# Value product of the attention from rounded parts, early products of the output projection, and a later output-weight load

## The reference, cut to what matters

```python
qkv = nodes @ Wqkv.T + bqkv                      # 512 x 2304
q, k, v = jnp.split(qkv, 3, axis=-1)             # 8 heads of 96
scores = jnp.einsum('nhd,mhd->hnm', q, k)        # q scaled by 96 ** -0.5
probs = jax.nn.softmax(scores, axis=-1)          # 8 x 512 x 512
attn = jnp.einsum('hnm,mhd->nhd', probs, v).reshape(n, D)
attended = attn @ Wo.T + bo
return nodes + attended                          # then x + this, layer norm, experts
```

## Time and profile before

| | us |
|---|---|
| three runs | 1343.64, 1342.67, 1346.37 (median 1343.64) |
| profiled execution, its own time | 1343.39 |
| span from its first to its last instruction | 1341.8 |
| mean granted TensorE clock in it | 0.989 |
| PE busy | 1276.1 (95%) |
| DVE busy | 918.2 (68%) |
| ACT busy | 589.3 (44%) |
| POOL busy | 127.7 (10%) |

### The profile page before, as it was taken

One profiled execution on the slowest core, in us unless ns is written; L12 is line 12 of the kernel. 1 busy time (PEld: TensorE's weight loads), 2 busy tenths in 40 slices (PEclk: granted clock), 3 DMA queues, 4 the chain that ended last, 5 costly groups with the idle time before them and its releaser, 6 DMA issues. The chain is left out here.

```text
span 1341.8 us, 19527 instructions
## 1 busy us (share of the span) xinstructions
PE 1276.1 (95%) x7089; PEld 1107.3 (83%) x7090; DVE 918.2 (68%) x1837; ACT 589.3 (44%) x1022; POOL 127.7 (10%) x123
## 2 busy tenths in 40 slices
PE   5999999999999999999999999999999898899997
PEld 4777569969969996666999999999998778796864
DVE  6477573473473475556759999999998778837524
ACT  3011141351351244235418888898886227502110
POOL 0000200000000000003320000000003018600101
PEclk9999999999999999999999999999999998999799
DMA  9421190410410620003257999999998300008134
GB/s 338 171 93 33 55 359 10 153 71 1 153 71 1 235 96 0 1 24 141 100 210 295 346 391 386 386 398 377 384 391 286 119 29 1 1 1 294 46 108 165
DMA packets 80704, 225.48 MB, mean 168 GB/s; under 512 B 5184, under 2 KB 17024, under 8 KB 80512
## 3 DMA queue, kind: packets, MB, share of 16 engines
q1 hardware_dynamic: 72736, 187.64, 37.8%
q0 software_dynamic: 7904, 36.97, 7.7%
HBM read 197.85 MB, written 26.74 MB: 167 GB/s over the span
## 5 line engine op out<-in xcount | busy, mean ns | idle before, releaser
L2149 DVE TENSOR_TENSOR part_slot<-slot,item_hi 128x768 fp32r<-128x768 f32 x150 | 133.1, 948 | 0.2
L1579 ACT ACTIVATE item_hi<-slot 128x768 fp32r<-128x768 f32 x156 | 118.0, 833 | 24.0 <-DMA slot<-in_e0w 22.5
L2158 DVE TENSOR_TENSOR part_slot<-slot,item_hi 128x768 fp32r<-128x768 f32 x132 | 116.5, 951 | 2.0 <-ACT item_hi L1587 1.5
L1587 ACT ACTIVATE item_hi<-slot 128x768 fp32r<-128x768 f32 x132 | 99.2, 831 | 13.9 <-DMA slot<-in_e0w 13.9
L731 PE MATMUL dve_ps<-item_hi,x_hi 128*128 128x384 f32 x288 | 99.3, 345 | 0.5 <-DVE x_lo L2338 0.3
L731 PE MATMUL act_ps<-item_hi,hid_hi 128*128 128x384 f32 x288 | 98.4, 342 | 0.3 <-DVE hid_lo L2350 0.3
L733 PE MATMUL dve_ps<-item_hi,x_lo 128*128 128x384 f32 x288 | 97.2, 337 | 0.0
L732 PE MATMUL act_ps<-part_slot,hid_hi 128*128 128x384 f32 x288 | 96.8, 336 | 0.0
L733 PE MATMUL act_ps<-item_hi,hid_lo 128*128 128x384 f32 x288 | 96.1, 334 | 0.0
L732 PE MATMUL dve_ps<-part_slot,x_hi 128*128 128x384 f32 x288 | 95.7, 332 | 0.0
L1470 ACT ACTIVATE h_t<-act_ps,par 128x256 f32<-128x256 f32 x36 | 21.1, 587 | 121.6 <-PE act_ps L849 121.6
(11 more groups left out here) (419 smaller groups left out, 3302.6 us busy)
## 6 DMA issues: line engine op xcount, KB each, us to landing
slot<-in_e0w SPq DMA_DIRECT2D x48, 2304.0 KB, 10.6
slot<-in_w SPq DMA_DIRECT2D x9, 2304.0 KB, 8.7
experts<-in_e1w SPq DMA_DIRECT2D x8, 1152.0 KB, 15.5
ea_raw<-in_edge SPq DMA_DIRECT2D x8, 1024.0 KB, 5.4
slot<-in_wqkv SPq DMA_DIRECT2D x3, 2304.0 KB, 13.7
xs<-zrow POOLq DMA_DIRECT2D x2, 3072.0 KB, 15.7
item_x<-xs SPq DMA_DIRECT2D x16, 384.0 KB, 9.7
ys<-item_y POOLq DMA_DIRECT2D x16, 384.0 KB, 6.9
```

The lines of the kernel that those rows point to most:

```text
L1579: go(item_hi[j][k][:, :], slot[s][:, k * D:(k + 1) * D], ACT.Copy).then_inc(up_high[j], 1)
L1587: go(item_hi[j][k][:, :], slot[s][:, k * D:(k + 1) * D], ACT.Copy).then_inc(down_high[j], 1)
L2149: vv.tensor_tensor(part_slot[s][:, ks], slot[s][:, ks], item_hi[j][k][:, :].bitcast(F32), ALU.subtract).then_inc(up_low[j], 1)
L2158: vv.tensor_tensor(part_slot[s][:, ks], slot[s][:, ks], item_hi[j][k][:, :].bitcast(F32), ALU.subtract).then_inc(down_low[j], 1)
```

## The change

1. The values are kept as two halves of four heads (`v`, in slot 0), rounded by ACT (`high_v`) and subtracted by DVE (`low_v`). The turned probabilities are also kept in parts: ACT copies all four banks into `prb_hi`, DVE subtracts that from the same bank into `prb_lo`, and it is DVE's subtraction that frees the bank. `weigh` makes 12 matmuls in fp32r in place of 4 plain ones, and waits bank by bank.
2. In heads 6 and 7 all four turned banks come from the ACT ring. The two `spend` calls there go. In head 6 PE makes 4 matmuls on ones and blocks 0 to 2 of unit 2, in head 7 blocks 0 to 2 of units 3 and 0, all ahead of `turn_probs`.
3. `high_attn`/`low_attn` of blocks 0 to 2 move into head 5 (behind ACT's four copies, behind DVE's `maxima(6)`).
4. `high_out` moves from behind the copies of the turned banks to right behind the exponentials of heads 5 and 6.
5. The whole output weight is loaded into slot 1 once query block 5 is made, in two pieces of 1152 KB; its rounded blocks lie in six places of their own (`wo_hi`).
6. `probs` has one buffer in place of two. Block 5 of the first expert's first half is rounded and subtracted last, after the output projection and after the norm.

```diff
-    HEAD_ACT, HEAD_DVE = HEAD_ACT + 2, HEAD_DVE + 2
+    HEAD_ACT, HEAD_DVE = (HEAD_ACT + 2, HEAD_DVE + 2) if _i < NH - 2 else (HEAD_ACT + NT, HEAD_DVE)
...
-            load(0, sview(0, 4, D), kview(wo[0:4 * P, :]))
...
             sp.wait_ge(sig.to_dve, DVE0["heads"] + HEAD_UNIT["q5"] + 1)
-            load(0, slot[0][:, 4 * D:DC * D].rearrange("p (k n) -> p k n", k=2), kview(wo[4 * P:DC * P, :]))
+            load(1, sview(1, DC, D)[:, 0:3, :], kview(wo[0:3 * P, :]))
+            sp.dma_start(sview(1, DC, D)[:, 3:DC, :], kview(wo[3 * P:DC * P, :])).then_inc(in_wo, 16)
...
             def turn_probs(i):
-                if i >= NH - 2:
-                    spend(act_bank(HEAD_UNIT[f"turn_a{i}"], a0), (10, 16)[i - NH + 2])
                 pe.wait_ge(prob_set, NT * (i + 1))
...
             def weigh(i):
-                pe.wait_ge(sig.act_freed, a0 + HEAD_UNIT[f"turn_a{i}"] + 2)
-                pe.wait_ge(sig.dve_freed, v0 + HEAD_UNIT[f"turn_v{i}"] + 2)
+                half, at = hd // 4, hd % 4 * DH
+                pe.wait_ge(v_low, half + 1)
                 for m in range(NT):
-                    last = mm(bank[0:DH, :], v[:, m, hd * DH:(hd + 1) * DH], prb_t[:, m, :], start=(m == 0), stop=(m == NT - 1))
+                    if i >= NH - 2:
+                        pe.wait_ge(sig.act_freed, a0 + HEAD_UNIT[f"turn_a{i}"] + m + 1)
+                    elif m % 2 == 0:
+                        pe.wait_ge(sig.act_freed, a0 + HEAD_UNIT[f"turn_a{i}"] + m // 2 + 1)
+                    else:
+                        pe.wait_ge(sig.dve_freed, v0 + HEAD_UNIT[f"turn_v{i}"] + m // 2 + 1)
+                    last = mm_parts(bank[0:DH, :], (v_hi[:, half, m, at:at + DH], v_lo[:, half, m, at:at + DH]),
+                                    (prb_hi[:, m, :], prb_lo[:, m, :]), start=(m == 0), stop=(m == NT - 1))
...
+                if i == NH - 2:
+                    spend(dve_ps[2], 4)
+                    pe.wait_ge(sig.dve_freed, v0 + HEAD_UNIT[f"turn_v{i - 1}"] + 2)
+                    attended(2, range(3), True)
+                if i == NH - 1:
+                    pe.wait_ge(sig.dve_freed, v0 + HEAD_UNIT[f"pv{i - 2}"] + 1)
+                    attended(3, range(3))
+                    pe.wait_ge(sig.dve_freed, v0 + HEAD_UNIT[f"pv{i - 1}"] + 1)
+                    attended(0, range(3))
                 turn_probs(i)
...
+            attended(2, range(3, DC - 1), True)
+            attended(3, range(3, DC - 1))
+            attended(0, range(3, DC - 1))
+            pe.wait_ge(sig.dve_freed, DVE0["wo"])
+            attended(used_last, range(DC - 1))
+            pe.wait_ge(wo_low, DC)
+            pe.wait_ge(attn_low, DC)
             for u in range(RING):
                 attended(u, range(DC - 1, DC)).then_inc(sig.to_dve, 1)
...
             for i in range(NH):
                 for t in range(NT):
...
+                if i in (5, 6):
+                    high_out(range(3 * (i - 5), 3 * (i - 4)))
                 for name in BETWEEN[i].split():
                     if name[0] == "k":
                         key(int(name[1]))
-                for j in range(2):
-                    go(prb_t[:, 2 * j, :], bank[:, :], ACT.Copy).then_inc(sig.act_freed, 1)
-                if i in (5, 6):
-                    high_out(range(3 * (i - 5), 3 * (i - 4)))
+                for m in range(NT):
+                    go(prb_hi[:, m, :], bank[:, :], ACT.Copy).then_inc(probs_high, 1)
+                if i == 0:
+                    high_v(1)
+                if i == 5:
+                    for k in range(3):
+                        high_attn(k)
...
-            for j in range(2):
-                high_up(j, 0)
+            high_up(0, 0, blocks=range(DC - 1))
+            high_up(1, 0)
+            act.wait_ge(sig.to_dve, DVE0["wo"] + 8)
+            high_up(0, 0, blocks=(DC - 1,))
...
             maxima(0)
+            low_v(0)
             for i in range(NH):
...
-                    vv.tensor_copy(prb_t[:, 2 * j + 1, :], bank[:, :]).then_inc(sig.dve_freed, 1)
+                for m in range(NT):
+                    dve.wait_ge(probs_high, NT * i + m + 1)
+                    vv.tensor_tensor(prb_lo[:, m, :], bank[:, :], prb_hi[:, m, :].bitcast(F32), ALU.subtract).then_inc(freed, 1)
                 if i + 1 < NH:
                     maxima(i + 1)
+                if i == 0:
+                    low_v(1)
+                if i == 5:
+                    for k in range(3):
+                        low_attn(k)
...
-            low_up(0, 0)
+            low_up(0, 0, range(DC - 1))
...
+            low_up(0, 0, (DC - 1,))
             keep_turned(run0, xn1_t)
...
                 pool.wait_ge(wo_high, k + 1)
-                nc.gpsimd.tensor_tensor(part_slot[0][:, ks], slot[0][:, ks], part_slot[1][:, ks].bitcast(F32), ALU.subtract
+                nc.gpsimd.tensor_tensor(part_slot[1][:, ks], slot[1][:, ks], wo_hi[k][:, :].bitcast(F32), ALU.subtract
```

More of the change, by code:

```diff
@@ L241, in build @@
         h_lo = over("h_lo", [P, DC, N], 18432, F32R)
-        v = over("v", [P, NT, D], 12288)
+        v = place("v", [P, 2, NT, HALF], F32, 0)
+        v_lo = place("v_lo", [P, 2, NT, HALF], F32R, 0)
+        v_hi = over("v_hi", [P, 2, NT, HALF], 12288, F32R)
         attn_t = over("attn_t", [P, DC, N], 6144)
@@ L257, in build @@
                  enumerate([3072, 3072 + D, cpt_at + 2 * N, area + 21504, area + 2048, bc_at])]
-        prb = over("prb", [P, 2, NT, N], 15360)
-        prb_t = over("prb_t", [P, NT, N], 19456)
+        prb = over("prb", [P, NT, N], 15360)
+        prb_lo = over("prb_lo", [P, NT, N], 17408, F32R)
+        prb_hi = over("prb_hi", [P, NT, N], 19456, F32R)
+        wo_hi = [place(f"wo_hi{k}", [P, D], F32R, at) for k, at in
+                 enumerate([3072, 3072 + D, 0, D, cpt_at + 2 * N, area + 22784])]
         xn1 = over("xn1", [P, NT, D], 0)
@@ new lines, in weigh, with attended @@
+                last.then_inc(sig.to_dve, 1)
+            def attended(u, ks, first=False):
+                t, half = u // 2, u % 2
+                ts, hs = slice(t * P, (t + 1) * P), slice(half * HALF, (half + 1) * HALF)
+                for k in ks:
+                    if first:
+                        pe.wait_ge(wo_low, k + 1)
+                        pe.wait_ge(attn_low, k + 1)
+                    last = mm_parts(dve_ps[u % RING][:, 0:HALF], (attn_hi[:, k, ts], attn_lo[:, k, ts]),
+                                    (wo_hi[k][:, hs], kslot(1, D, True)[:, k, hs]), start=(k == 0), stop=(k == DC - 1))
+                return last
@@ L1533, in _, with high_v @@
                 go(part_slot[3][:, k * D:(k + 1) * D], slot[2][:, k * D:(k + 1) * D], ACT.Copy).then_inc(w_high, 1)
+            def high_v(half):
+                act.wait_ge(sig.dve_freed, DVE0["v"] + 7 + half)
+                go(v_hi[:, half, :, :], v[:, half, :, :], ACT.Copy).then_inc(v_high, 1)
+            high_v(0)
             def key(b):
@@ L1559, in _, with high_up @@
                         key(int(name[1]))
-                for j in range(2):
-                    bank = bank_of(HEAD_UNIT[f"turn_a{i}"] + j, a0)
-                    wait(act, sig.to_dve, DVE0["heads"] + HEAD_UNIT[f"pv{i - 1}"] + 1 if i else 0)
-                    go(prb_t[:, 2 * j, :], bank[:, :], ACT.Copy).then_inc(sig.act_freed, 1)
-                if i in (5, 6):
-                    high_out(range(3 * (i - 5), 3 * (i - 4)))
-            act.wait_ge(sig.to_act, ACT0["heads"] + HEAD_UNIT["k5"] + 1)
-            for k in range(DC):
-                act.wait_ge(sig.dve_freed, DVE0["heads"] + HEAD_UNIT[f"pv{NH - 2 if k < DC - 1 else NH - 1}"] + 1)
-                go(attn_hi[:, k, :], attn_t[:, k, :], ACT.Copy).then_inc(attn_high, 1)
-            def high_up(j, i, home=None, before=0):
+                wait(act, sig.to_dve, DVE0["heads"] + HEAD_UNIT[f"pv{i - 1}"] + 1 if i else 0)
+                for m in range(NT):
+                    if i >= NH - 2:
+                        bank = bank_of(HEAD_UNIT[f"turn_a{i}"] + m, a0)
+                    elif m % 2 == 0:
+                        bank = bank_of(HEAD_UNIT[f"turn_a{i}"] + m // 2, a0)
+                    else:
+                        act.wait_ge(sig.to_dve, DVE0["heads"] + HEAD_UNIT[f"turn_v{i}"] + m // 2 + 1)
+                        bank = dve_ps[(HEAD_UNIT[f"turn_v{i}"] + m // 2) % RING]
+                    go(prb_hi[:, m, :], bank[:, :], ACT.Copy).then_inc(probs_high, 1)
+                if i == 0:
+                    high_v(1)
+                if i == 5:
+                    act.wait_ge(sig.to_act, ACT0["heads"] + HEAD_UNIT["k5"] + 1)
+                    for k in range(3):
+                        high_attn(k)
+            for k in range(3, DC):
+                high_attn(k)
+            def high_up(j, i, home=None, before=0, blocks=range(DC)):
                 s = run0.up_slots[j]
                 act.wait_ge(run0.w_in[s], 16 * (i + 1))
-                for k in range(DC):
+                for k in blocks:
                     if home is not None:
```

(2 more changed lines are left out.)

68 lines of the change are left out of this document (38 added, 30 removed).

## The result

The changed kernel takes 1348.35 us (median of 20 runs, 1344.34 to 1352.19) against 1343.53 us for the kernel before, 20 runs beside them. The ratio is 1.0034, with a 95% interval from 1.0022 to 1.0045: slower by 0.34%, where 1338.7 us and most likely faster was forecast. The profiled execution has a span of 1344.9 us, 3.1 more than before's 1341.8.

The account below looks back on a forecast made before the run. PE was taken to bound until head 5, a PE-ACT-DVE loop heads 6 and 7, then DVE's start on the first unit; -3.3 + 0.2 + 1.3 - 0.4 - 5.7 + 3.1 = -4.8 us gave 1338.7 us, range 1335 to 1348.5.

Parts of the forecast that it names:

- Part 1: Value product, heads 0 to 4: twelve fp32r matmuls replace four plain ones, 0.66 us saved per head, -3.3 us in sum.
- Parts 2 and 3: Divisions of heads 5 and 6: each waits once for POOL, then DVE does all four multiplications; distances 12.3 and 12.7 us.
- The terms +0.2 and +1.3: Forecast delays from POOL holding the division: PE loses 0.2 us in head 5, head 6's distance grows 1.3 us.
- Part 4: Head 6's turning to head 7's: division ends at 12.45 us against 12.94 before, early matmuls fit in, -0.4 us.
- Part 5: Last head's turning to the projection's first addition: 11.7 us instead of 17.4, -5.7 us.
- Part 6: Norm after the projection: its chain meets four POOL instructions instead of two, PE stays ahead, +3.1 us.
- rival A: Strict turns: POOL takes the port after each multiplication in heads 5 and 6; 1347.4 to 1350 us, chance 0.25.
- B: PE's 2.7 us idle before head 6's turning costs the clock once: +2.5 us, 1341.2 us, chance 0.12.
- C: Less holding: POOL's blocks come later or multiplications are not held; 1337.8 us, or 1335.5 with the norm's old share; chance 0.14.
- D: The change does not reach the end, a later load bounds what follows: about 1343 us, chance 0.04.

Follow-up runs that it names:

- experiment 1: Changed kernel with ACT's roundings of the output weight moved back behind those of the turned probabilities in heads 5 and 6: 1344.31 us.
- experiments 5: Changed kernel with output weight rounded behind the probabilities, without early projection products and early attention rounding: 1340.96 us.
- 9: Changed kernel with late output-weight rounding, no early products or early attention rounding, and DVE making POOL's six expert subtractions later: 1338.81 us.
- 10: Changed kernel with late output-weight rounding, attention roundings in head 6, 27 early products before head 7's turning, DVE making POOL's expert subtractions later: 1334.04 us.
- experiment 2: Changed kernel with 16 more products of ones while PE waits for the norm's third tile: 1348.39 us.
- the third experiment: Changed kernel with POOL's six expert-weight subtractions started only after DVE has scaled the norm's first two tiles: 1351.16 us.

## Why the prediction was wrong, step by step

**Part 1, the value product: right.** In head 4 twelve matmuls start 0.23 us apart from about 595.8 and the next projection begins at 598.56; the turnings of heads 1 to 4 follow at 16.3 or 12.1 us instead of 16.9 to 17.0 and 12.8. The turning of head 4 is 2.8 us earlier, and without a collision that of head 5 comes after 12.10 us (forecast 12.3). No bank was late there.

**Parts 2 and 3, the divisions of heads 5 and 6: the failed step.** It is the sentence "I take it that DVE, whose multiplications stand ready one behind the other, then does all four". POOL started at 599.08, 8.5 us after the turning of head 4, where 8.7 was forecast; the place was right and the handover wrong. The terms +0.2 and +1.3 measured +2.9 (14.99 against the 12.10 of an undisturbed head) and +4.6 (15.93 against 11.36), the second with 3.4 us at half clock in it, from 606.2 to 609.6. The rows of before gave a sign: after the tiny operation of 0.91 us the very next one took 1.77, and POOL's last subtraction had begun in between the earlier trace rows. Had DVE kept the port once it had it, the second one would have taken 0.17. It was no proof, since each tiny operation stands behind a wait and the multiplications do not, but I read the first of the pair and not the second.

The Trainium skill (SBUF — State Buffer, Who interferes with whom) says that the engine that issues first holds the shared ports for its whole instruction. The trace agrees: the first two held multiplications end at 601.22 and 603.21, behind the POOL instructions in front of them, which end at 600.93 and 602.92.

**Part 4, head 7: right.** 12.83 us against 12.5.

**Part 5, first addition: right in its length** (11.84 against 11.7), late by what the two heads lost: 646.20 instead of 640.0, so 1.7 us earlier than before and not 7.9.

**Part 6, the norm: right in what it counted, wrong in what it left out.** Four held operations were forecast at +3.1, and four were held. What was left out is the second failed step: "PE has only just begun unit 4 and stays ahead" was taken as harmless. PE stays so far ahead that it runs dry while DVE is held, half clock follows, and the products of ones ahead of the last tile hold that tile up: 34.12 us against 26.36 is +7.8, where the sum had +3.1. The rows on PE's idle of 4.63 us and the half clock behind it were used in rival A for the heads alone; nobody asked them of the norm. A step that is won by one engine and held on the next is an idle of the first.

**The sum.** At the logits the profile stands at -1.7 + 7.8 = +6.1 us. It is still +6.2 at 1154 us; in this one execution 3 us come back after 1250 us, where the kernel before ran 13.7 us at half clock and this one two times 3.4. The medians differ by 4.8. Two figures of the working are off by little: 1338.6 + 0.25 is 1338.8 and not 1338.7, and the early products of head 6 fill about 2.5 us (four products on ones 0.9, nine of 0.176), which leaves an idle of 2.2 us and not 2.7.

**The rivals.** A gave the mechanism and nearly the time (1347.4 to 1350, measured 1348.35); its distances 15.85 and 15.5 stand against 14.99 and 15.93. But it had 0.25, and its time came near partly by luck: it left out the norm's clock, and it priced 2.5 us for each clock loss in the heads, once or twice, where one stretch of 3.4 us at half clock, a loss of 1.7 us, is seen. B, a clock loss behind PE's idle in the heads, is a part of what happened, at another place: it put it ahead of head 6's turning, where an idle of 3.62 us was followed by full clock, and it came behind the idle of 2.73 us ahead of head 5's. C and D did not happen.

## What to carry to other kernels

Two streams of short instructions from SBUF to SBUF on DVE and POOL did not share in any run here: each of DVE's waited for one whole instruction of POOL. So count the pairs that meet and price each at POOL's length, whatever DVE's own is. Moving POOL's stream only pays if it goes to where DVE works from PSUM (its maxima took 0.69 us each beside POOL in the kernel before, as alone) or does nothing; otherwise shorten its instructions, or let DVE do the work when it is idle (0.88 us a block instead of up to 1.8 lost). And where a change makes the feeding engine earlier and the next one later, price the idle in between, clock included, and with it every product that only fills time and stands ahead of real work (2.92 us at full clock here, 5.42 at half).

## What was not expected of the hardware

- The turns are strict in every meeting seen: 2.0 us per multiplication held for a whole instruction of POOL's 768 columns, 1.2 for one of 384, 2.3 per 512-wide subtraction (experiment 1), 1.73 to 1.78 for operations on 128x1 or 128x2 elements that take 0.16 alone. POOL pays too, but less: three of its subtractions take 5.35 us alone in the kernel before, 5.42 with one multiplication met (experiments 5, 9, 10), 5.79 beside the division, 6.30 beside DVE's three subtractions.
- Half clock came behind an idle of 4.05 us in the norm (10.2 us at 0.50), and with PE's wait filled (experiment 2) it did not come there. But the idle alone does not tell: in the heads 2.73 us was followed by half clock, 3.62 us was not, and 3.63 us in the third experiment was.
- A second stretch at half clock stands around the logits with PE busy ahead of it and in it, within or just behind the last tile's narrow products (128x8): 3.4 us from 674.5 in the kernel before, 6.8 from 677.8 in the changed one, 6.8 from 675.0 with the wait filled. What brings it there no run shows. The clock of a kernel with such waits moves from place to place, and a gain of 3 us at one place need not reach the end.
